# One stage for the second feed-forward: nine expert units per block, weighted before the down projection and summed in PSUM

## What is computed

```python
logits = flat @ router_w.T
topk_scores, topk_idx = jax.lax.top_k(logits + router_bias, 2)
topk_scores = jax.nn.softmax(topk_scores, axis=-1)
combine = zeros((N, 16)).at[arange(N)[:, None], topk_idx].add(topk_scores)
up_all = einsum('nd,kde->nke', flat, up_proj)        # k experts of 64 hidden values
gate_all = einsum('nd,kde->nke', flat, gate_proj)
hidden = silu(gate_all) * up_all
down_all = einsum('nke,ked->nkd', hidden, down_proj)
out = einsum('nk,nkd->nd', combine, down_all)
sh_hidden = silu(flat @ sh_gate.T) * (flat @ sh_up.T)   # shared expert, 128 hidden values
out = out + sh_hidden @ sh_down.T
# x = x + tanh(g) * out, with flat = layernorm(x)
```

## Time and profile before

| | us |
|---|---|
| median of 3 executions (range) | 1620.95 (1615.14 to 1621.0) |
| profiled execution, its own time | 1605.87 |
| its span, first to last instruction | 1604.0 |
| TensorE busy | 1258.0 |
| VectorE busy | 760.8 |
| ScalarE busy | 612.2 |
| GpSimd busy | 434.1 |
| mean granted TensorE clock | 0.833 of full |

### The profile page before, as it was taken

How to read it: one execution, slowest core, us unless ns; L and a number is a source line. 1 busy time by engine, 2 the same in 40 slices (tenths; PEclk the granted TensorE clock), 3 DMA queues, 4 the chain that set the end, 5 groups by cost and what they waited for, 6 DMA issues and landing times. The chain is left out here.

```text
span 1604.0 us, 29425 instructions
## 1 busy us (share of the span) xinstructions
PE 1258.0 (78%) x9544; PEld 884.9 (55%) x9544; DVE 760.8 (47%) x3253; ACT 612.2 (38%) x1533; POOL 434.1 (27%) x628
## 2 busy tenths in 40 slices
PE   5988783999599999589977736857677999984384
PEld 3766562677356666355646636845444555454274
DVE  4655364233386764457744440132445677436012
ACT  3544341332486763211123303333141566621253
POOL 2665216233045452000005163420000000004443
PEclk8999895899799999799978757976655899965597
DMA  6696201230799000000000115640033222030153
GB/s 180 192 215 198 93 9 45 72 102 18 116 120 171 26 1 1 6 26 16 0 14 2 53 52 141 176 114 1 1 157 62 52 58 61 17 119 18 50 154 83
DMA packets 141384, 119.97 MB, mean 75 GB/s; under 512 B 13092, under 2 KB 120539, under 8 KB 141256
## 3 DMA queue, kind: packets, MB, share of 16 engines
q1 hardware_dynamic: 126376, 99.26, 26.8%
q0 software_dynamic: 7824, 15.32, 3.6%
q10 hardware_dynamic: 7056, 3.81, 0.9%
HBM read 80.63 MB, written 40.72 MB: 76 GB/s over the span
## 5 line engine op out<-in xcount | busy, mean ns | idle before, releaser
L306 POOL TENSOR_TENSOR L_Z<-L_Z,L_mx 128x512 f32<-128x512 f32 x84 | 88.5, 1054 | 324.0 <-DVE L_mx L617 324.0
L2955 DVE TENSOR_REDUCE L3s_mx<-L3s_psS 128x1 f32<-128x512 f32 (+3 forms) x256 | 107.7, 483 | 42.6 <-PE L3s_psS L2849 39.2
L908 ACT ACTIVATE L_Z<-L_Z,L_nmx 128x154 f32<-128x154 f32 x256 | 105.1, 414 | 42.6 <-DVE L_nmx L965 42.5
L2921 ACT ACTIVATE L3s_E<-L3s_psT 128x512 f32<-128x512 f32 (+1 forms) x192 | 87.9, 531 | 54.2 <-PE L3s_psT L2862 54.0
L740 POOL TENSOR_TENSOR L_Z<-L_Z,L_rin 128x488 f32<-128x488 f32 x64 | 64.0, 1000 | 124.8 <-DVE L_rin L973 124.8
L2827 POOL COPY L3s_VG<-L3s_V 128x236 f32 x16 | 7.6, 480 | 322.6 <-PE L3s_psO L2873 173.6
L617 DVE CUSTOM_DVE_ANT_0 L_Z<-L_psS,L_Z 128x154 f32<-128x154 f32 x256 | 63.5, 316 | 61.0 <-PE L_psS L354 51.7
L808 PE MATMUL L_psS<-L_G,L_xnT 128*128 128x462 f32 x192 | 82.4, 525 | 2.8 <-DVE L_nmx L965 1.4
L1382 DVE SCALAR_TENSOR_TENSOR X<-L1f_psY,comb,X 128x128 f32<-128x128 f32 x256 | 72.3, 344 | 23.9 <-PE L1f_psY L1340 18.6
L2847 PE MATMUL L3s_psS<-L3s_KS,L3s_QS 72*128 72x512 bf16 (+3 forms) x256 | 66.6, 335 | 9.5 <-DMA L3s_KS<-k_parts 8.3
L965 DVE CUSTOM_DVE_ANT_0 L_Z<-L_psS,L_mask 128x154 f32<-128x154 f32 x256 | 67.7, 314 | 11.4 <-PE L_psS L808 10.9
(11 more groups left out here) (559 smaller groups left out, 3125.2 us busy)
## 6 DMA issues: line engine op xcount, KB each, us to landing
L_Z<-in_fside_Bx16xSxS SPq DMA_DIRECT2D x16, 1232.0 KB, 9.3
L2f_w<-in_L_ffn_W SPq DMA_DIRECT2D x39, 256.0 KB, 2.8
slotsL<-empty SPq DMA_DIRECT2D x1, 8320.5 KB, 77.8
L3f_w<-in_L_ffn_fc_w SPq DMA_DIRECT2D x32, 256.0 KB, 3.8
L0f_w<-in_L_ffn_W SPq DMA_DIRECT2D x24, 256.0 KB, 4.2
q_parts<-L3s_parts SPq DMA_DIRECT2D x3, 1536.0 KB, 8.9
L3s_QS<-q_parts SPq DMA_DIRECT2D x16, 288.0 KB
L3s_KS<-k_parts SPq DMA_DIRECT2D x48, 96.0 KB
```

The costliest lines, as they stand in the source:

```text
L306: nc.gpsimd.tensor_tensor(Z[:, t % NZ, h, 0:KM_], Z[:, t % NZ, h, 0:KM_], top.broadcast_to([P, HG, KM_]), ALU.subtract).then_inc(z_ready, 1)
L908: last = nc.scalar.activation(Z[:, t % 2, h], Z[:, t % 2, h], ACT.Exp, scale=-1.0, bias=nmx[:, t % 2, h:h + 1], accum_out=sums[:, t % 2, h ...
L2921: nc.scalar.activation(E[:, g.par, h, EO[group[0]]:EO[group[0]] + wd], psT[:, k, 0:wd], ACT.Exp).then_inc(t_free, 1)
L2955: last = nc.vector.tensor_reduce(mx[:, t, h:h + 1], psS[:, k, at:at + wd], AX_X, ALU.max)
```

## The change

The three stages become one, `mixture` ("L1m"). The statistics of each tile are taken in the attention stage, right after the tile's `residual` (`measure`, `gather`), into `m.st1` and `m.mv1`. The stage has 4 blocks x 9 units (p = 0 is the shared expert, 1 to 8 the pairs), 36 units n. TensorE issues `hidden(n)` for all n and, 17 units later (LAG), `outputs(n - 17)`. An output is now one product of 128 rows and 512 columns with the down weights stationary; the nine of a block are summed in one PSUM bank, with features on partitions. Then ScalarE copies the sum (`keep_sum`), TensorE turns it back (`turn_back`), and VectorE adds it times the gate to `m.X` (`residual`, 4 in all). Each token's weight must therefore be on the hidden values before the product: VectorE multiplies `h` by `cb` (`scale`, 32 in all, 15 units behind `gate`). `cb` holds the weights of one block, copied over 64 partitions for each expert of a pair: the weights are turned (`turn_comb`), copied to SBUF, written to DRAM (32 KB a block) and read back by two DMAs of 1 MB each, twice buffered, all on the queue of SyncE. The router's steps are spread between VectorE's gatings, its first part after unit 1, the second after unit 4, the last after unit 10. `h` is a ring of 19 tiles, and all weights of the stage are loaded at its start.

```diff
@@ wide_attention, vector engine
+            def measure(t):
+                dve.wait_ge(y_free, t + 1)
+                own.done(nc.vector.bn_stats(m.st1[:, t], m.X[:, t]))
+
+            def gather(t):
+                own.wait()
+                own.done(nc.vector.bn_aggr(m.mv1[:, t], m.st1[:, t]))
...
                     if g == 3 and 0 <= y < NT:
                         residual(y)
+                    if g == 4 and 0 <= y < NT:
+                        measure(y)
+                    if g == 5 and 0 <= y < NT:
+                        gather(y)
...
+def mixture(nc, m, name, c):
+    NE, HR, LAG, BACK, E = 9, 19, 17, 15, 16
+    N = TB * NE
+    groups = [(0, 1), (1, 3), (3, 6), (6, 9)]
...
+            for k in range(TB):
+                sp.wait_ge(t_done, TB + k + 1)
+                sp.dma_start(comb_rows[k], combT[:, k]).then_inc(rows_out, 16)
+                sp.wait_ge(rows_out, 16 * (k + 1))
+                if k >= 2:
+                    sp.wait_ge(scaled, 8 * (k - 1))
+                pairs = comb_rows[k].rearrange("(e a) t -> a e t", a=2)
+                for a in range(2):
+                    sp.dma_start(cb[64 * a:64 * a + 64, k % 2], pairs[a:a + 1].broadcast_to([64, 8, 512])).then_inc(cb_in[k % 2], 16)
+        @block.tensor
...
+                if n >= 2:
+                    pe.wait_ge(a_free, n - 1)
+                pe.matmul(psA[:, n % 2], w1[:, p], x, start=True, stop=True).then_inc(a_full, 1)
+                if n >= 2:
+                    pe.wait_ge(b_free, n - 1)
+                pe.matmul(psB[:, n % 2], w3[:, p], x, start=True, stop=True).then_inc(b_full, 1)
...
+                if p == 0:
+                    pe.wait_ge(b_free, n + 1)
...
+                else:
+                    pe.wait_ge(scaled, 8 * k + p)
+                pe.matmul(psY[:, k % 2], w2[:, p], h[:, n % HR], start=(p == 0), stop=(p == NE - 1)).then_inc(y_full, 1)
...
+            turn(0)
+            turn(1)
+            hidden(0)
+            turn(2)
+            turn(3)
+            hidden(1)
+            logits()
+            for n in range(2, N):
+                hidden(n)
+                if n >= LAG:
+                    outputs(n - LAG)
+                if n == 12:
+                    turn_comb(0)
+                    turn_comb(1)
+                if n == 13:
+                    turn_comb(2)
+                    turn_comb(3)
+                k, p = divmod(n - LAG, NE)
+                if p == 1 and k >= 1:
+                    turn_back(k - 1)
+            for n in range(N - LAG, N):
+                outputs(n)
+                k, p = divmod(n, NE)
+                if p == 2 and k >= 1:
+                    turn_back(k - 1)
+            turn_back(TB - 1)
...
+            def scale(n):
+                k, p = divmod(n, NE)
+                if p == 0:
+                    return
+                if p == 1:
+                    dve.wait_ge(cb_in[k % 2], 32 * (k // 2) + 32)
+                dve.wait_ge(b_free, n + 1)
+                nc.vector.tensor_tensor(h[:, n % HR], h[:, n % HR], cb[:, k % 2, p - 1], ALU.mult).then_inc(scaled, 1)
...
+            for n in range(N):
+                gate(n)
+                if n == 1:
+                    choose_first()
+                if n == 4:
+                    choose_second()
+                if n == 10:
+                    combine()
+                if n >= BACK:
+                    scale(n - BACK)
+                k, p = divmod(n - LAG, NE)
+                if p == 2 and k >= 1:
+                    residual(k - 1)
+            for n in range(N - BACK, N):
+                scale(n)
+                k, p = divmod(n, NE)
+                if p == 5 and k >= 2:
+                    residual(k - 1)
+            residual(TB - 1)
...
-    norm_transpose(nc, m, "L1r", m.X, m.XN, router=dict(E=16, kind="L1", w=w["L1_ffn_router_w"][:], gate=5, comb=m.comb[:]))
-    experts(nc, m, "L1s", dict(w1=d["L1_ffn_sh_gate"], w3=d["L1_ffn_sh_up"], w2=d["L1_ffn_sh_down"], act=ACT.Silu,
-                               dst=m.X, share=lambda *a: m.gate(5)))
-    experts(nc, m, "L1f", dict(w1=d["L1_ffn_gate_proj"], w3=d["L1_ffn_up_proj"], w2=d["L1_ffn_down_proj"], act=ACT.Silu,
-                               dst=m.X, share=share(16, 2), split=2))
+    mixture(nc, m, "L1m", dict(sh_w1=d["L1_ffn_sh_gate"], sh_w3=d["L1_ffn_sh_up"], sh_w2=d["L1_ffn_sh_down"], w1=d["L1_ffn_gate_proj"],
+                               w3=d["L1_ffn_up_proj"], w2=d["L1_ffn_down_proj"], wr=w["L1_ffn_router_w"][:], gate=5))
```

More of the change, by code:

```diff
@@ L1049, in _ @@
                     last.then_inc(t_full, 1)
-            if router:
-                r.tensor(pe, xt_ready)
         @block.vector
@@ L1274, in _ @@
             clear_last(m, sp)
[L1275 to L1283 removed]
+            for g, (lo, hi) in enumerate(groups):
+                for dst, shared, routed in ((w1, c["sh_w1"], c["w1"]), (w3, c["sh_w3"], c["w3"])):
+                    src = shared if lo == 0 else routed[lo - 1:hi - 1]
+                    sp.dma_start(dst[:, lo:hi], src.rearrange("e p f -> p e f")).then_inc(wa_in[g], 16)
@@ new lines, in _ @@
+            for n in range(1, N):
+                silu(n)
+                if n == 9:
+                    act.wait_ge(diff_ready, 1)
+                    nc.scalar.activation(v[:, 3], v[:, 2], ACT.Exp).then_inc(exp_ready, 1)
+                if n == 12:
+                    keep_comb(0)
+                    keep_comb(1)
+                if n == 13:
+                    keep_comb(2)
+                    keep_comb(3)
+                k, p = divmod(n - LAG, NE)
+                if p == 0 and k >= 1:
+                    keep_sum(k - 1)
@@ L1355, in _ @@
+            for k in range((N - LAG) // NE, TB):
+                keep_sum(k)
         @block.vector
         def _(dve):
[L1357 to L1388 removed]
@@ new lines, in _, with step, gate @@
+            own = Own(dve, own_v)
+            wide = lambda a: a.unsqueeze(2).broadcast_to([P, NT, E])
+            order = m.const["rank16"].unsqueeze(1).broadcast_to([P, NT, E])
+            def step(ins):
+                own.done(ins)
+                own.wait()
+            def gate(n):
+                dve.wait_ge(a_free, n + 1)
+                dve.wait_ge(b_full, n + 1)
+                nc.vector.tensor_tensor(h[:, n % HR], h[:, n % HR], psB[:, n % 2], ALU.mult).then_inc(b_free, 1)
+            def scale(n):
+                k, p = divmod(n, NE)
+                if p == 0:
+                    return
[3 more added lines that the diff above has]
+                nc.vector.tensor_tensor(h[:, n % HR], h[:, n % HR], cb[:, k % 2, p - 1], ALU.mult).then_inc(scaled, 1)
@@ new lines, in residual @@
+            def residual(k):
+                dve.wait_ge(back_full, k + 1)
+                x = m.X[:, k * TB:(k + 1) * TB].rearrange("p t d -> p (t d)")
+                nc.vector.scalar_tensor_tensor(x, psL[:], m.gate(c["gate"]), x, ALU.mult, ALU.add).then_inc(back_done, 1)
+            dve.wait_ge(std_ready, 1)
+            step(nc.vector.reciprocal(rs[:], std[:]))
+            for k in range(TB):
+                for t in range(k * TB, (k + 1) * TB):
+                    last = nc.vector.tensor_scalar(m.XN[:, t], m.X[:, t], m.mv1[:, t, 0:1], rs[:, t:t + 1], ALU.subtract, ALU.mult)
+                last.then_inc(x_ready, 1)
```

400 lines of the change are left out of this document (113 added, 287 removed).

## The result

The kernel with the change takes 1560.41 us, median of 4 executions (1557.34 to 1563.24), beside 1618.05 (1610.22 to 1621.0) for the kernel before in the same session: a ratio of 0.9651, interval 0.9605 to 0.9696. The profiled execution took 1557.76 with a span of 1556.0, against 1604.0 before. Of 1618.05 us the interval makes 49 to 64 us. The medians differ by 57.6 us, the profiled spans by 48.0.

A forecast was written before the change was run, and what follows sets the result against it. It took TensorE to bound the loop, with serial preparation and low-clock restarts filling the rest of the 168.3 us stage. 815.2 - 762.3 - 1.4 = 51.5 us saved; 1620.95 - 51 = 1570 us, own range 1562 to 1578, outer 1558 to 1590.

The forecast's parts named there:

- Output product and unit: Loop of units: the output becomes one product of 0.86 us, so a unit takes 2.58 us instead of 3.56.
- Attention: Statistics moved into attention: hidden in its body, 0 us (bounds 0 and 4.8); the last tile's pair adds 0.45 us.
- Start: Stage start: TensorE's first turn at 650.75 us, after attention ends at 647.35; `hidden(0)` at the lower clock takes 3.44 us.
- Logits: After `hidden(1)` in the stage's start: the logits take 4.35 us and end at 663.5 us.
- Units 2 to 16: Hidden units beside the router's chain: 15 x 1.72 us, 1.0 lost to the chain, four weight turns at 0.6: 29.2 us.
- Copied weights: Wait in `scale(1)` for block 0's 2 MB: 10 us to land, 2 us lost (bounds 0 and 13); later blocks no wait.
- (a): Rival, chance 0.19: copies at 19.4 us for 2 MB, block 0 10 us late, TensorE restarts low; +20, 1590 us.
- Semaphores of the next stage: Stage end: 27 semaphores to clear instead of 11 before layer 2's first weights, costing 1.4 us.
- (b): Rival, chance 0.04: four copy transfers in series make it slower than before; threshold 27.5 us each, 1730 us at 55.0.
- (c): Rival, chance 0.06: the router's selection still stops TensorE, 8.5 us instead of 1.0 and a low restart of 3; 1581 us.
- (d): Rival, chance 0.04: a unit stays near 3.5 us because ScalarE and VectorE hand over too late; 1587 us.
- weighing of turns and the clock: Stage start: turns taken to raise TensorE's clock; by the skill's rule `hidden(1)` and second turns would cost 2.8 us more.

The follow-up runs named there:

- before_wide8: Kernel before, with one 128-row, 512-column output product in place of eight small ones, the 8 additions kept: 1588.51 us, stage 148.48.
- no_copies_late: Changed kernel without the copies of the tokens' weights, `cb` filled with ones by GpSimd after the normalising: 1548.69 us, stage 112.77.
- before_wide4: Kernel before, with one wide output product in place of eight small ones and 4 additions instead of 8: 1560.31 us, stage 129.68.
- copies_twice: Changed kernel with both copies of each block made a second time after the first pair landed: 1585.28 us, stage 156.10.
- logits_spread: Changed kernel with the 16 logit products in four groups between hidden units and the first two selection parts moved later: 1548.69 us, stage 114.34.
- chain_whole: Changed kernel with the router's chain in one piece after unit 1 and the weights turned after unit 3: 1560.52 us, stage 115.99.
- pool_scale: Changed kernel with the 32 scalings moved from VectorE to GpSimd: 1561.18 us, stage 120.22.

## Why the prediction was right

The forecast was 1570 us with a range of 1558 to 1590; the time is 1560.41. That is inside the range, by 2.4 us, but outside of 1562 to 1578, to which I gave 0.66 for my own mechanism. The stage came out 2.3 us longer than forecast and the total 9.6 us shorter, so two errors pull against each other, and that the range held is in part luck. The sum was made for the profiled execution, and there it stands better: a stage of 115.4 us against 117.66, a span of 1552.5 against 1556.0. The 9.6 us between forecast and median come mostly from the step that carried the sum over: I took the offset of 15 us between the median and the profiled execution of before as one that stays. Its profiled execution (1605.87) was quicker than all four executions of the comparison (1610.22 and up); after, the offset is 2.65. Two profiles of single executions give a difference that is off by such a spread. The second session has 56.4 us between the medians (1612.94 and 1556.56), so the gain is nearer to 57 than to the 50.6 of the stage. In which part of the kernel the other 6 us lie no profile shows, since there is only one of the kernel before and it is of a quick execution.

The terms, in the order of the prediction:

- *Output product and unit*: 2.58 us forecast, 2.58 measured, and TensorE busy 39.00 of 39 us. `before_wide8` shows that this needed the additions gone.
- *Scaling on VectorE*: 0.68 forecast, 0.684 measured, idle 0.0 before it and hidden beside 2.58.
- *Attention*: 0 in the body and 0.45 in the tail forecast; 0.2 and 0.55 (650.35 to 650.90) measured.
- *Start*: first turn 3.85 us after attention forecast, 3.93 measured; first hidden product 5.95 forecast, 5.87 measured; `hidden(0)` at the low clock 3.44 forecast, 3.00 (656.22 to 659.22) measured.
- *Logits*: the end was 16.6 us after attention in the forecast and 14.95 in the trace. The step that was mis-sized is 4.35 us for the logits, taken whole from the earlier trace rows. That row held a fall of the clock that I had not opened; unslowed they take 3.5 (661.81 to 665.30).
- *Units 2 to 16*: 29.2 forecast, 665.30 to 695.80 = 30.5 measured. The selection's stalls were 0.25 after `choose_second`, 0.09 at the exponential and 0.86 before `turn_comb`, 1.2 against the 1.0 taken; four turns were 0.435 each instead of 0.6. What was not in the sum is the low clock behind the logits, 1.8 us. "I charge the lower clock once" failed: it was charged three times, at the start, after the logits and after the wait for the copies.
- *Copied weights*: the term that was furthest off. Issued 39.7 us after attention (40.1 forecast), but 12.9 us to land, not 10, and the restart that I had priced only in rival (a). 2 us were taken, the bounds were 0 and 13, and `no_copies_late` measures 4.9. The nearest row would have been the 11.9 for 2 MB; I had chosen the middle by size and packets. That row is a write to DRAM (`q_parts` lies there), which the prediction counted among the loads, so its closeness may be chance; and the 19.4 of the slow row should read 77.8 x 2048 / 8320.5 = 19.2. Blocks 1 to 3 need no wait, as forecast; block 3 has 0.96 us on VectorE that stays hidden, so 13 us for 2 MB is the edge.
- *Tail*: 17 outputs at 0.86 us and the last turn and addition as forecast.
- *Semaphores of the next stage*: +1.4 forecast, +0.88 measured (1.77 against 0.89).

These errors sum to -1.65 for the logits' end, +1.3 for units 2 to 16 and +2.9 for the copies: 115.4 + 2.55 = 117.95, beside the 117.66 of the trace. Of the gain of 50.6 us, 38.6 come with the narrow output products and the additions (`before_wide4`), more than the 31 of 32 units x 0.98, since a wait in the middle of the old loop went too, and 12.0 from one stage in place of three, net of the copies.

On the rivals: (a) had the right mechanism for what was lost, at a third of its size. (b) was brought about in `copies_twice` by twice the bytes; its walk through four transfers in series holds, with its threshold somewhat above 27.5 us, since at 26 us the stage was still 12 us shorter than before. (c) and (d) did not come. On the weighing of turns and the clock: `hidden(1)` and the second pair of turns ran at full clock (0.60 us for four turned tiles at 659.22), so the 2.8 us by the Trainium skill's rule on transposes, as the prediction gives it, did not come. That doesn't refute the rule, since `hidden(0)` stood between.

## What to carry to other kernels

A wider product pays only as far as the engine that empties PSUM keeps up: count what VectorE does per unit before and after, and let PSUM do the summing where a scaling can be moved ahead of the product. A transfer on the way between two stages must be dated at both ends, when its source is ready and when its buffer is free; delaying the consumer mends the first wait and can open another where the work per unit gets shorter, while a first half with its own semaphore mends it without that. When a duration is lifted from a row, look at the granted clock inside it first.

## What the runs showed of the hardware

- A run of 16 float32 products of 16 columns lowered the granted clock from 1.00 to 0.50 with TensorE busy throughout, for 3.2 us in the kernel after and already in the kernel before; so in eleven traces of eleven. The same products in four portions between wide ones did not, in three of three.
- A wait of TensorE of 3.31 us left the granted clock at 1.00 (`logits_spread`), while one of 2.87 us (`chain_whole`) and one of 3.09 us (kernel before) were followed by 0.50.
- A fill of 128 x 4096 float32 values by GpSimd doubled VectorE's normalising beside it, 8.39 instead of 4.19 us for 16 steps that read and write SBUF, while the same fill (`no_copies_late`) and multiplications on GpSimd (`pool_scale`) left VectorE's gating, one operand of which is in PSUM, at 0.69. The Trainium skill (GPSIMD Engine Reference, Key points) says that GpSimd shares its SBUF interfaces with VectorE and contends with VectorE's two-port modes and two-input steps from SBUF; both observations agree with that as far as they go, but in which mode the normalising ran no trace shows.
- A float32 multiplication of 128 x 512 values took 1.27 us on GpSimd and 0.68 on VectorE.
- Two DMAs of 1 MB, each copying 8 rows of 2 KB in DRAM to 64 partitions, took 12.9 us from issue to use, 163 GB/s; nearly the same with twice the bytes in series (13 us per 2 MB).
